# Key reads of a fused transformer block issued from two engines' queues instead of one

## The reference

```python
x = x + xattn(layernorm(x), ctx, ctx)    # q,k,v projections, softmax over 1601 keys
x = x + gated_attn(layernorm(x))         # 16 heads, sigmoid of cosine similarity
x = x + ffn(layernorm(x))                # top-1 of 8 experts
```

## Time and profile before

| | |
|---|---|
| time, median of 3 runs | 333.4 us (333.14 to 334.82) |
| the profiled execution | 333.99 us, its span 332.3 us |
| PE busy | 301.6 us, 91% |
| DVE, ACT, POOL busy | 161.2, 90.7, 78.4 us |
| split reads (FF from ctx) | 80 DMAs of 128 KB and 32 of 256 KB, all from SP |
| DMA queues | q1, from SP, carries 69.23 of 74.27 MB |

### The profile page before, as it was taken

The page is one execution under the profiler, slowest core; times in us unless marked ns, Lnnn a source line. Parts: engine busy times, 40 slices in busy tenths (PEclk is TensorE's granted clock), DMA queues, the critical chain, the costliest instruction groups (busy, mean ns, idle before and its releaser), DMA issues. The chain is left out here.

```text
span 332.3 us, 5209 instructions
## 1 busy us (share of the span) xinstructions
PE 301.6 (91%) x1806; PEld 159.8 (48%) x1806; DVE 161.2 (49%) x364; ACT 90.7 (27%) x209; POOL 78.4 (24%) x84
## 2 busy tenths in 40 slices
PE   0999899999899889999989999999998989899792
PEld 0788567643454544445455445455543344443330
DVE  3303338537263763828185833738561354735431
ACT  1132230235112346321234442124411013411110
POOL 5000003167022500112340020135102246103202
PEclk9999999999999999999999999999999999999998
DMA  7999999999999998999949699952715996153300
GB/s 250 390 374 172 184 311 387 211 187 257 387 211 228 279 187 132 375 250 227 324 77 192 116 393 220 258 204 83 298 63 145 396 411 266 28 205 109 119 2 34
DMA packets 61364, 74.27 MB, mean 224 GB/s; under 512 B 3187, under 2 KB 40083, under 8 KB 60320
## 3 DMA queue, kind: packets, MB, share of 16 engines
q1 hardware_dynamic: 59792, 69.23, 80.2%
q0 software_dynamic: 1552, 4.78, 4.0%
HBM read 70.85 MB, written 3.67 MB: 224 GB/s over the span
## 5 line engine op out<-in xcount | busy, mean ns | idle before, releaser
L1251 PE MATMUL SC<-CT_sb,QC_sb 128*64 128x256 f32 x384 | 50.4, 389 | 0.3 <-DVE CT_sb L847 0.2
L847 DVE STREAM_TRANSPOSE CT_sb<-FF_sb 128x1024 f32<-128x1024 f32 x36 | 42.4, 1220 | 14.3 <-DMA FF_sb<-ctx 12.7
L1290 PE MATMUL ST<-CTX_sb,PR_sb 128*64 128x512 f32 (+1 forms) x208 | 48.2, 600 | 1.1 <-ACT PR_sb L347 1.1
L1251 PEld LDWEIGHTS SC<-CT_sb,QC_sb 128*64 128x64 f32 x384 | 24.7, 136 | 17.2 <-issue 9.0
L1176 PE MATMUL A<-AW_sb,normT_sb 128*128 128x512 f32 x64 | 29.4, 599 | 1.3 <-DVE normT_sb L918 1.3
L1290 PEld LDWEIGHTS ST<-CTX_sb,PR_sb 128*64 128x64 f32 (+1 forms) x208 | 13.9, 136 | 23.2 <-issue 22.3
L532 POOL TENSOR_TENSOR rn_sb<-ss_sb,nhalf_sb 128x16 f32<-128x16 f32 x4 | 11.7, 2915 | 33.9 <-DVE ss_sb L923 33.9
L1176 PEld LDWEIGHTS A<-AW_sb,normT_sb 128*128 128x128 f32 x64 | 11.7, 190 | 14.8 <-issue 12.2
L1169 PE MATMUL TR<-ident_sb,CTX_sb 128*128 128x128 f32 (+1 forms) x128 | 16.1, 266 | 2.3 <-DVE CT_sb L340 1.1
L1196 PE MATMUL A<-AW_sb,WQK_sb 128*128 128x256 f32 x64 | 16.4, 422 | 0.8 <-ACT AW_sb L645 0.8
L1169 PEld LDWEIGHTS TR<-ident_sb,CTX_sb 128*128 128x128 f32 (+1 forms) x128 | 12.9, 141 | 8.7 <-issue 5.6
(11 more groups left out here) (227 smaller groups left out, 459.0 us busy)
## 6 DMA issues: line engine op xcount, KB each, us to landing
CTX_sb<-ctx SPq DMA_DIRECT2D x24, 1024.0 KB, 10.7
FF_sb<-ctx SPq DMA_DIRECT2D x80, 128.0 KB, 7.2
FF_sb<-ctx SPq DMA_DIRECT2D x32, 256.0 KB, 7.9
CTX_sb<-wgu SPq DMA_DIRECT2D x4, 1024.0 KB, 9.4
CTX_sb<-wdn SPq DMA_DIRECT2D x5, 512.0 KB, 12.8
FF_sb<-wgu SPq DMA_DIRECT2D x2, 1024.0 KB, 6.6
rows<-XR_sb SPq DMA_DIRECT2D x3, 512.0 KB, 10.7
CTX_sb<-ctx SPq DMA_DIRECT2D x8, 130.0 KB
```

The costliest lines, as they stand in the source:

```text
L847: v.transpose(ctxT[:, pos % 2, k, :, :].rearrange("p c (b r) -> p b c r", r=Q), split[:, k, at:at + BLOCKS, :].rearrange("p b (c r) -> p b ...
L1251: last = t_.matmul(out[q, :], (qcurP if split_group else qcur)[:, c, q], ctxT[:, pos % 2, k, c, 0:n], start=(c == 0), stop=(c == DC - 1))
L1290: last = t_.matmul(ST[q, :], probs[0:w, t, q], ctxb[0:w, k, t, :], start=(t == 0), stop=(t == KT - 1))
```

## The change

The first two parts of pair 0 stay with SP. Every later part is cut in two: SP issues the lower partition quarters (`LOWER`, quads 0 and 1, 4 DMAs a part), where it issued the whole part, and ACT issues the upper ones (`UPPER`, quads 2 and 3), at places of its own instruction list: parts 0 and 1 of pair 1 behind the exponentials of pair 0; parts 2 and 3 of pair p in step u = 1 of pair p; part 1 of pair p+1 in step u = 5; part 0 of pair p+1 behind the move of c = 0 in `sums(p)`. Each has the wait on `keysT_made` that SP has.

```diff
+UPPER_REST, UPPER_FIRST = 1, 5
...
+        def load_split(eng, p, part, quads):
+
+            first, slot = SPLIT_PARTS[part][0] * GT * P, SLOT_OF[SPLIT_PARTS[part][0]]
+            n = len(SPLIT_PARTS[part]) * BLOCKS
+            for quad in quads:
+                for k in range(2):
+                    src = A["ctx"][bass.ds(2 * p + k, 1), first:first + n * Q, quad * P:(quad + 1) * P]
+                    eng.dma_start(split[quad * Q:(quad + 1) * Q, k, slot * BLOCKS:slot * BLOCKS + n, :],
+                                  src.rearrange("a (b r) d -> r (a b) d", r=Q)).then_inc(s_split[part], 16)
...
                 sp.wait_ge(s["keysT_made"], split_turned(p, order_of(p).split.index(3) + 1))
                 settle(sp)
-                load_split(p + 1, 1)
+                load_split(sp, p + 1, 1, LOWER)
                 sp.wait_ge(s["keysT_made"], split_turned(p, len(order_of(p).split)))
                 settle(sp)
-                load_split(p + 1, 0)
+                load_split(sp, p + 1, 0, LOWER)
...
-                load_split(p, 2)
-                load_split(p, 3)
+                load_split(sp, p, 2, LOWER)
+                load_split(sp, p, 3, LOWER)
...
+            def upper_first(p, n, part):
+
+                act.wait_ge(s["keysT_made"], split_turned(p, n))
+                if not isinstance(p, int):
+                    settle(act)
+                load_split(act, p + 1, part, UPPER)
+
+            def upper_rest(p):
+
+                act.wait_ge(s["keysT_made"], split_turned(p, 2))
+                settle(act)
+                load_split(act, p, 2, UPPER)
+                load_split(act, p, 3, UPPER)
...
             exponentials(0)
+            upper_first(0, 2, 0)
+            upper_first(0, 3, 1)
             move_qk(False, 2)
             move_qk(False, 3)
...
                     move_keys(act, a.copy, p, 0, NEXT.tile(u))
+                    if u == UPPER_REST:
+                        upper_rest(p)
+                    if u == UPPER_FIRST and not is_last(p):
+                        upper_first(p, NEXT.split.index(3) + 1, 1)
                 exponentials(p)
...
                 move_numerators(act, a.copy, p, 0)
+                if not is_last(p):
+                    upper_first(p, len(NEXT.split), 0)
```

More of the change, by code:

```diff
@@ L347, in move_numerators @@
             copy(probs[0:w, lo:hi, :], TR[c % 2][0:w, 0:(hi - lo) * P].rearrange("p (t q) -> p t q", q=P)).then_inc(s[f"moved{c % 2}"], 1)
+        def load_split(eng, p, part, quads):
[6 more added lines that the diff above has]
+                                  src.rearrange("a (b r) d -> r (a b) d", r=Q)).then_inc(s_split[part], 16)
+        LOWER, UPPER = range(QUADS // 2), range(QUADS // 2, QUADS)
         @block.sync
@@ L359, in load_ctx @@
                     sp.dma_start(ctxb[0:TAIL, k, FULL, :], src).then_inc(s_ctx[k][c], 16)
[L361 to L369, removed]
             def next_split(p):
@@ L374, in next_split @@
                     sp.wait_ge(s["keysT_made"], split_turned(0, 2))
-                    load_split(1, 0)
+                    load_split(sp, 1, 0, LOWER)
                     sp.wait_ge(s["keysT_made"], split_turned(0, 3))
-                    load_split(1, 1)
+                    load_split(sp, 1, 1, LOWER)
                     return
@@ L429, in _ @@
                 load_chunk(0, c)
-            load_split(0, 0)
-            load_split(0, 1)
+            load_split(sp, 0, 0, range(QUADS))
+            load_split(sp, 0, 1, range(QUADS))
             sp.wait_ge(s["qp_made"], 2 * DC)
```

## The result

The changed kernel takes 349.96 us, median of 4 runs (347.87 to 352.06), where the kernel before takes 333.27 beside it (4 runs, 332.4 to 334.82). The ratio is 1.0495, 95% interval 1.042 to 1.0571, some 16.5 us. The direction was forecast, the size was not: 339.5 us was predicted, 344.0 was the top of the range. The profiled execution took 352.06 us, its span is 350.3 us, 18.0 more than before. All ratios here leave out executions over 1.5% above the fastest of their kernel, so they are not always the ratio of the two medians given.

The account below looks back on a forecast made before the run. PE was taken as the bound. The terms 3.2 - 1.8 + 2.2 + 2.5 = +6.1 us on the profiled 333.99 gave 340.1 us, stated as 339.5 us for the median of runs; range 334.3 to 344.

Parts of the forecast that it names:

- Start, +3.2: End of pair 0: eight ACT issues ahead of its first move make PE wait 3.2 us more.
- D: Time the eight ACT issues at the start take: 8 x 0.50 plus 0.4 us for sharing, 4.4 us.
- Pair 1's late reads, -1.8: Pair 1: PE's waits for a late chunk read and a late DVE result go, giving back 1.8 us.
- Parts 2 and 3, 0: Step u = 1: eight ACT issues, 4.0 us, fit an idle gap of 4.57 us and cost nothing.
- rival D: ACT's issues held up with SP's: start costs up to 10.1 us, u = 1 overruns; 346 us and more, chance 0.13.
- Part 1, 0: Step u = 5: four ACT issues, 2.0 us, data not needed until the next pair, no cost.
- Part 0, +2.2 and +2.5: Sums of pairs 1 and 2: the next pair's upper part 0 lands late, delaying DVE; PE loses 2.2 and 2.5 us.
- Chunk 0's sharing: Part 0's reads share with SP's chunk 0 of the next pair, adding 0 to 1 us, taken as 0.5.
- A: Rival: ACT issues almost for free, reads run at 387 GB/s, pair 1's lateness comes back; 331.8 us, chance 0.05.
- B: Rival: only the start stalls, part 0's upper half lands within some 5.5 us; +1.0, 334.4 us, chance 0.12.
- C: Rival: only data are late; ACT's start issues run during its exponentials or cost little; +2.9, 336.3 us, chance 0.14.
- The rule beside it: Two concurrent DMAs to the two partition halves gain 6%, since all run on the same DMA engines; sum unchanged.

Follow-up runs that it names:

- the kernel of 30 products: Changed kernel plus 30 identity matmuls, result unused, on PE ahead of its wait for ACT's first move: 344.89 us, ratio 1.0329 to the kernel before.
- part0_only: Kernel before with only the upper quarters of part 0 of pairs 2 and 3 issued by ACT, behind the move of c = 0: 341.96 us, ratio 1.0237.
- ahead: Changed kernel, but ACT issues pair 1's part 0 before waiting on c_made, later part 0 before the exponentials; SP issues pair 1's part 1: 332.79 us, ratio 0.999.
- rest_only: Kernel before with only the upper quarters of parts 2 and 3 issued by ACT, at u = 1: 334.62 us, ratio 1.0026.
- part0_early: start_sp with ACT's part 0 issued ahead of the exponentials instead of behind the move of c = 0: 335.91 us, ratio 1.0063 to the kernel before.
- start_sp: Changed kernel with parts 0 and 1 of pair 1 wholly from SP again, loop as changed: 341.0 us, ratio 1.0183 to the kernel before.

## Why the prediction was wrong in size

**Start, +3.2.** Here it failed. The step said that ACT's queue is empty then and took D = 4.4 us; D was some 8.1 (the copies have 8.10 us of issue ahead of them), and PE lost 6.9 (7.16 against 0.24), which is D - 1.2 as the step had it. The path was right, its price was not. "Empty" was true and not enough: four reads of 256 KB went in at the empty queue's price, hidden under the exponentials, and the fifth was held for 4.71 us, until about when the first landed (64.86 + 6.7 = 71.6). How much a queue takes before it holds the engine is not settled. Here it was 1 MB, and at u = 1 of pair 1 eight reads of 128 KB, 1 MB again, passed without a hold. At u = 1 of pair 2 six of them passed in 0.4 us each and the last two took 1.93 and 2.44; the seventh was let go at 159.4, before any of them had landed (the first at 162.1). The prediction had both ends, 3.7 to 4.0 and 11.3, and chose by the queue instead of by the DMA engines behind it, which still had SP's reads in hand: from 64.8 to 67.4 us all 922 packets that moved, 175 GB/s, were of SP's queue, and none was ACT's. How much of the 3.7 us by which D was too small is SP's traffic, and how much ACT's own 1.5 MB, no run tells apart.

**What the wait does to the clock, not in the sum.** 2.3 us at the start, and 6.7 us of pair 2's start at half clock, behind waits of 1.66 and 0.81 us. With PE kept busy the dip at the start is gone in both profiles and the kernel of 30 products is some 5 us faster (1 to 10), so there PE's idling brings it. For pair 2 this is not shown: `part0_only` has nearly the same waits at full clock.

**Pair 1's late reads, -1.8.** Right: no wait for a chunk in the changed kernel, 2.2 us in `ahead`. In the changed kernel it is buried under the late part 0.

**Parts 2 and 3, 0.** Right by itself (`rest_only` 1.0026) and in pair 1 of the changed kernel (3.92 us in the gap of 4.57). In pair 2 eight issues took 7.76 us and cost PE 1.15, the case that rival D named. **Part 1, 0:** right, 1.9 us each time.

**Part 0, +2.2 and +2.5.** Mechanism and place right, by `part0_only` (3.4 and 2.6) and by `part0_early`, which takes it away. The term of pair 1 was sized too small: the reads landed 8.9 instead of 7.7 + 0.5 us after the first issue, and ahead of PE stand also the query copies of ACT (0.81 us at 150.81), which the sum took for free. Chunk 0's sharing was priced at 0.5 us; it made the last 50 packets wait, as the rows of pair 1 show.

**Rival D** (0.13) said ACT would be held up with SP's issues. Half of it came: ACT is held. But not with SP: while ACT's fifth issue was held from 66.92 to 71.63, SP issued at 68.75 in its usual time.

```profile
68.75 0.39 SPq L410 DMA_DIRECT2D AO_sb<-awo  x1
```

So SP had room while ACT had none; what they share is the DMA engines behind the queues. **A** (0.05) and **B** (0.12) fell: the issues were not free, and part 0's upper half landed 8.9 and 7.9 us after its first issue. **C** (0.14) said that ACT's issues run while its exponentials compute: so did four of the eight.

**The rule beside it** (the Trainium skill, SBUF — State Buffer, "Can I just issue two DMAs to hit both halves?", 6%) put the halves at next to nothing. The trace of `start_sp` differs: 274 to 280 GB/s by halves against 187 for one queue. On the sum it changed nothing, since what hurt was when the reads went out.

**The sum:** +0.4, start +6.9, half clock there +2.3, pair 1 +0.6 (relief and late part 0 together), pair 2 +5.0 (about 2.7 of half clock by its eight-matmul rows and the stretch's length, 1.15 held ACT, the rest rank and the query copies), rest +2.8: 18.0. Of the 11.9 us beyond the forecast 3.7 are D and some 5 the clock; 1.15 is ACT held in pair 2. PE's busy time, 7.5 us longer for the same instructions, is another measure of the clock: 2.3, 2.7 and 1.7 by the three stretches, 0.8 unassigned. In the rest after pair 2 stand 1.07 us for step on, which the forecast had within its 2.5, and another stretch of half clock near the end (330.5 to 333.9), which is not traced to the change. The prediction's own range was added up a little too wide: D = 6 and sharing of 1 us a time make 342.1, not 342.5.

## What to carry to other kernels

A DMA issue on ACT cost 0.4 to 0.5 us here until its queue held the engine, 4.71 us for one issue. Price it by how much the queue already holds and by what the DMA engines have in hand, and put it where the engine idles and owes nobody, as `ahead` does. Data that wait for a place in such an engine's list are late by that place: count landing from there, and follow the wait to what is queued behind it. A wait of several us on PE cost its length and then half clock on top (7.16 us, and 2.3 more).

## What the runs showed of the hardware

Reads spread over both queues landed far out of order. The third and fourth of ACT's reads at the start, a window that holds those two issues:

```profile
L358 ACTq DMA_DIRECT2D FF_sb<-ctx x2: 509/510/510, 65.8 to 66.4; - x2
...
DMA to landing us min/median/max: 9.2/12.5/15.9
```

The one took 9.2 us, the other, issued half a microsecond later, 15.9, until 82.26, which is when DVE's turn of part 0 began (82.27, after 8.07 us of waiting). A stretch with split reads on one queue and chunk reads on the other:

```profile
105.00:111.00 6.00, 6.00 (x17) 2.66 (x15) 2.71 (x4) 0.69 (x1) 0.00 (x0) 1.00 1.09 327
```

In these 6 us SP's queue moves 793 packets, 1.58 MB, and ACT's 762, 0.37 MB: packets of 2 KB and of 512 bytes pass about one for one. So the chunks have some 263 of the 327 GB/s, where they alone move 387. The second queue with its small pieces takes half of the packets and gives a fifth of the bytes.
